# Adaptive layer norm block on one core: second half's means on 32-column tiles of TensorE, and the fifth product's operand prepared one step earlier

## The chip, the cores and the metric

The kernel is written in Bass and runs on one core of one Trainium2 chip. Everything is float32 in memory; the large products run in fp32r on pieces of the operands (high part and rest), the small ones in float32. The metric is the time of one execution on the device, in microseconds (us), the median of a few runs.

## The reference

```python
def reference(L0_attn_x, L0_ffn_W_gate, L0_ffn_W_up, L0_ffn_W_down, L0_c, L0_wmod):
    # x (2, 2048, 1024), W_gate and W_up (2752, 1024), W_down (1024, 2752), c (2, 1024), wmod (1024, 6144)
    x = L0_attn_x
    mod = (_silu(L0_c) @ L0_wmod).reshape(L0_c.shape[0], 6, 1, -1)
    sa, ca, ga, sb, cb, gb = (mod[:, 0], mod[:, 1], mod[:, 2], mod[:, 3], mod[:, 4], mod[:, 5])
    ga = (2 * (ga >= 0) - 1) * jnp.maximum(jnp.abs(ga), 0.25)
    gb = (2 * (gb >= 0) - 1) * jnp.maximum(jnp.abs(gb), 0.25)
    h = _layernorm(x, axis=-1) * (1 + ca) + sa
    x = x + ga * _L0_attn_ref(h)      # attention between the 2 batch rows, per channel, over the positions
    h = _layernorm(x, axis=-1) * (1 + cb) + sb
    x = x + gb * _L0_ffn_ref(h, L0_ffn_W_gate, L0_ffn_W_up, L0_ffn_W_down)   # silu(h Wg') * (h Wu'), then Wd'
    return x
```

The attention scores of a channel are sums over all 2048 positions, so the first layer norm has to be done for the whole of x before anything behind it can start.

## The kernel before

**Stages.** x lies with its features on the partitions and is cut into 8 chunks of 512 tokens (256 positions of both batch rows), 8 feature tiles of 128 each. Stage one normalises all chunks and gathers the sums for the attention; it takes four pairs of chunks in turns `t` = 0 and 1, each turn with pair `u` = 0 and 1 and chunk `h` = 0 and 1 of the pair. Stage two works out the attention's coefficients, applies them to the first two chunks, normalises again and makes the operands of the feed-forward part. Stage three, which is over nine tenths of the time, is the feed-forward part: products `P1` to `P7` of Strassen's scheme, each for two tiles of output features (`u` 0 and 1), three fp32r matmuls for each (high by high, high by rest, rest by high), then the down projection in the same manner. Every engine has its own program in written order; semaphores tie them together, so nothing is reordered.

**Stage one, turn t.** For a chunk, TensorE sums over the features by multiplying with ones, so that the mean stands on all 128 partitions (`means`, L1564: 8 float32 matmuls of 512 columns in turn 1). VectorE subtracts it (`centre`, L986, two instructions per chunk), ScalarE squares (`square`, L669), TensorE sums the squares on tiles of 32 columns, four quarters of the chunk side by side (`variances`, L1577), ScalarE takes the root (`root`, L677), VectorE the reciprocal (`invert`, L991), TensorE spreads it back over the partitions (`spread`, L1587, four matmuls with `rows_of`), VectorE multiplies (`normalise`, L1003) and takes the cross products (L1012), ScalarE the sums of squares of the result (`square_sums`, L686). VectorE's order in a turn is centre (0,0), (0,1), (1,0), invert (0,0), centre (1,1), invert (0,1), then the normalising of pair 0 and pair 1.

**Queues.** The sync engine (SP) issues the loads on queue q1: x, and the 24 parts of 1 MB of the modulation weights (`wmod`), which go through a ring of three buffers. Part w is loaded as soon as part w-3 has been multiplied (`parts`, L1535; `load_part`, L371). ScalarE issues the stores of the normalised chunks on its own queue q10 (`save_xhat`, L661), four halves of 2 MB in turn 0. Before it overwrites pair 1's buffer in turn 1, VectorE's centre (1,0) waits for the two stores of that pair (`xh_stored[1]`), and for all sums of squares of turn 0 (`sqsum_done`).

**The start of stage three.** The first pass takes the products in the order P1, P1, P2, P2, P5, P5, P6, P6, ... The operands of P1 and P2 are blocks of the normalised input (`raw_b11`, `raw_b21`), those of P5, P7, P6 and P4 sums of blocks. ScalarE makes the blocks of the second chunk (`modulate_f(1, k)`, L754, k 0 to 3 and then 4 to 7) and the high parts (`x_hi_first`, L794), VectorE the sums (L1220, L1224, L1231, L1234) and the rests (`x_lo_part`, L1193).

Of the kernel before, what the change touches and what calls it, by code (L numbers as in the profile page):

```python
# [20 lines left out]
F32 = mybir.dt.float32  # L21
# [4 lines left out]
P = 128  # L26
# [4 lines left out]
KD = D // P  # L31
KH = KD // 2
# [15 lines left out]
PRESUM = 4  # L48
NTB = T // P
# [81 lines left out]
def build(nc, x, xp, wgu, wgn, wdn, cT, eye, wmod, out):  # L131
# [3 lines left out]
    def sb(name, shape, dt, at):  # L135
        return nc.alloc_sbuf_tensor_at(name, [P] + shape, dt, offset=base + at)


    xbuf = [sb("xbuf0", [2, KD, NB, CC], F32, 32 * K), sb("xbuf1", [2, KD, NB, CC], F32, 64 * K)]
    dbuf = [sb("dbuf0", [2, KD, NB, CC], F32, 96 * K), sb("dbuf1", [2, KD, NB, CC], F32, 0)]  # L140
    rows_first = sb("rows_first", [2, BLOCK], F32, 140 * K)
    presum = sb("presum", [2, T], F32, 180 * K)
    presums = [presum, sb("presum1", [2, T], F32, 144 * K)]
# [120 lines left out]
    std_ready, inv_ready, rstd_ready = sem("std_ready"), sem("inv_ready"), sem("rstd_ready")  # L264
    xh_stored = [sem(f"xh_stored{u}") for u in range(2)]
    xhat_ready, sqsum_done, cross_done = sem("xhat_ready"), sem("sqsum_done"), sem("cross_done")
    wm_loaded = [sem(f"wm_loaded{r}") for r in range(WM_RING)]
    wm_last_loaded = sem("wm_last_loaded")
    silu_ready, mod_done = sem("silu_ready"), sem("mod_done")
# [47 lines left out]
    def tok(ap):  # L317

        return ap.rearrange("p k b c -> p k (b c)")
# [40 lines left out]
    with block as block:  # L360
# [281 lines left out]
        def _(act):  # L642
# [13 lines left out]
            for t in range(NPAIR // 2):  # L656
                def save_xhat(u, half):

                    act.wait_ge(xhat_ready, t * (4 * KD) + 2 * KD * u + KD * (half + 1))
                    first, ks = 4 * t + 2 * u + 2, slice(half * KD // 2, (half + 1) * KD // 2)  # L660
                    s.dma_start(xhat_dram[first:first + 2].rearrange("h p (k w) -> p h k w", k=KD)[:, :, ks],  # L661
                                tok2(dbuf[u][:, :, ks])).then_inc(xh_stored[u], 16)

                def square(u, h, js):
                    i = 2 * u + h
                    for j in js:
                        act.wait_ge(centred, t * 8 + (2 * i + j * 2 // NSQ + 1))
                        act.wait_ge(sq_used, t * (4 * NSQ) + (i * NSQ + j + 1))
                        s.activation(sq[:, j % 2], tok(dbuf[u][:, h])[:, j * SQ_PER:(j + 1) * SQ_PER, :], ACT.Square).then_inc(  # L669
                            sq_ready, 1)  # L670

                def root(u, h):
                    i = 2 * u + h
                    act.wait_ge(sq_used, t * (4 * NSQ) + (i * NSQ + NSQ + 2))
                    if t:
                        act.wait_ge(inv_ready, i + 1)
                    s.activation(std[:, u, h, :], ps_mean[u][h][:, 0:P], ACT.Sqrt, bias=eps_t, scale=1.0 / D).then_inc(std_ready, 1)  # L677

                def square_sums(u, ks):
                    for k in ks:  # L680
                        for b in range(NB):
                            n = 2 * u * KD + NB * k + b
                            act.wait_ge(xhat_ready, t * (4 * KD) + (n + 1))

                            act.wait_ge(sqsum_done, t * (4 * KD) + (4 * KD + n - 1))
                            s.activation(junk_a[:, b], dbuf[u][:, :, k, b, :], ACT.Square,  # L686
                                         accum_out=part[:, u, 2 + b, k:k + 1]).then_inc(sqsum_done, 1)

                for u, h in ((0, 0), (0, 1), (1, 0), (1, 1)):
                    square(u, h, range(NSQ // 2))  # L690
                    if (u, h) != (0, 0):
                        root(u if h else 0, 1 - h)
                    square(u, h, range(NSQ // 2, NSQ))
                root(1, 1)
                square_sums(0, range(KD // 2))
                save_xhat(0, 0)
                square_sums(0, range(KD // 2, KD))
                save_xhat(0, 1)
                if t:
                    copy_rows(0)  # L700
                square_sums(1, range(KD // 2))
                if t == 0:
                    save_xhat(1, 0)
                square_sums(1, range(KD // 2, KD - 2))
                if t:
                    copy_rows(1)
                square_sums(1, range(KD - 2, KD))
                if t == 0:
                    save_xhat(1, 1)
# [39 lines left out]
            def modulate_f(h, k):  # L749

                act.wait_ge(tf_ready, KD * h + k + 1)
                to = ((raw_b11, raw_b21), (x_raw["P6"], x_raw["P3"]))[h][k // KH]
                for n in range(NB):
                    ins = s.activation(to[:, k % KH, n * CC:(n + 1) * CC], xh_f[:, h, k, n, :], ACT.Identity,  # L754
                                       bias=mod[:, 3, n, k:k + 1], scale=cb1[:, n, k:k + 1])
                ins.then_inc(rawf_ready, 1)
# [26 lines left out]
            copy_rows(3)  # L783
            for m in range(4, EARLY):
                w_hi_cast(m)
            for k in range(KH, KD):
                modulate_f(1, k)

            def x_hi_first(name):

# [3 lines left out]
                s.copy(x_hi[name][:], x_raw[name][:]).then_inc(xhi_ready, 1)  # L794

            x_hi_first("P5")

            def silu_c11(g, u):

# [166 lines left out]
        def _(dve):  # L966
# [253 lines left out]
            v.tensor_tensor(x_raw["P5"][:], x_raw["P6"][:], raw_b11[:], ALU.subtract).then_inc(sumsf_ready, 1)  # L1220
            w_lo_part(3)
            w_lo_part(4)
            dve.wait_ge(rawf_ready, 2 * KD)
            v.tensor_tensor(x_raw["P7"][:], x_raw["P3"][:], x_raw["P6"][:], ALU.subtract).then_inc(sumsf_ready, 1)  # L1224
            x_lo_part(0, "P5")

            def x_first(i):

# [288 lines left out]
        def _(pe):  # L1517
# [36 lines left out]
            for t in range(NPAIR // 2):  # L1554
                def means(u, h):
                    i = 2 * u + h
                    pe.wait_ge(x_half, 16) if t == i == 0 else pe.wait_ge(x_loaded[u][h], t * 16 + 16)
                    if t and u == 0:
                        pe.wait_ge(std_ready, i + 1)
                    if t and u == 1:  # L1560
                        pe.wait_ge(xhat_ready, 2 * KD)
                    bank, ks = ps_mean_late[h] if t and u else ps_mean[u][h], range(KD) if t else range(PRESUM, KD) if i else range(KH)
                    for k in ks:
                        ins = mm(bank, ones[:], tok(xbuf[u][:, h])[:, k, :], start=k == ks[0], stop=t == 1 and k == KD - 1)  # L1564
                    if t == 0:
                        pe.wait_ge(presum_ready, i) if i else pe.wait_ge(half_ready, 2)
                        ins = mm(bank, ones[:], presums[u][:, h, :], start=False, stop=True)
                    ins.then_inc(mean_mm, 1)

                def variances(u, h):  # L1570
# [16 lines left out]
                        ins = mm(ps[:, RSTD_BANK[u] + h, b * P:(b + 1) * P], rows_of[:, b, :], inv[:, u, h, :], start=True, stop=True)  # L1587
                    ins.then_inc(rstd_ready, 1)

                means(0, 0)  # L1590
                means(0, 1)
                if t == 0:
                    means(1, 0)
                    variances(0, 0)
                    means(1, 1)
# [9 lines left out]
                    spread(1, 1)  # L1605
                    parts(0, range(2, 3))
                else:
                    means(1, 0)
                    means(1, 1)
                    parts(0, range(3, GROUP[0]))  # L1610
                    variances(0, 0)
                    variances(0, 1)
# [226 lines left out]
```

## Time and profile before

| | us |
|---|---|
| median of 3 runs | 2700.56 (2700.24 to 2702.29) |
| profiled execution | 2705.58 |
| its span | 2703.8 |
| TensorE busy in it | 2632.3 |
| VectorE busy | 1787.1 |
| ScalarE busy | 1303.8 |

The span runs from the first to the last instruction of the profiled execution, which took 1.78 us longer in all. Its own time is 5.02 us above the median of the unprofiled runs. TensorE is busy for 97% of the span. The exceptions lie in the first 215 us, stages one and two and the first products, where TensorE, VectorE, ScalarE and the transfers wait for each other.

### The profile page before, as it was taken

How to read it: one execution, taken by the hardware profiler on the slowest of the kernel's cores; microseconds unless marked ns; L12 is line 12 of the kernel's file. 1: busy time of each engine (PE TensorE's matmuls, PEld its weight loads, DVE VectorE, ACT ScalarE, POOL GpSimd, SP SyncE). 2: the span in 40 equal slices, each digit the busy share in tenths (PEclk: the TensorE clock that was granted, in tenths of full speed). 3: DMA queues.
4: the chain of work that ended last, by engine and by line, in shares of the span. 5: the costliest groups of instructions: out<-in, count | busy, mean ns of one | idle time of the engine just before them, and what ended most of it. 6: DMA issues, size and time to landing. Idle time of an engine off the chain costs nothing.

```text
span 2703.8 us, 34116 instructions
## 1 busy us (share of the span) xinstructions
PE 2632.3 (97%) x12264; PEld 2134.6 (79%) x12264; DVE 1787.1 (66%) x2505; ACT 1303.8 (48%) x2058; POOL 112.4 (4%) x176
## 2 busy tenths in 40 slices
PE   7779999999999999999999999999999999999999
PEld 3447888887888888888887888888888888888887
DVE  7898787758677757677757656667455555555544
ACT  5575555646555646456655333334333433343332
POOL 2000011010011010011000000000000000000000
PEclk9889999999999999999999999999999999999999
DMA  9764666567566557666559787778666667657655
GB/s 404 281 269 152 191 223 225 183 210 246 176 225 226 192 182 261 196 225 226 165 175 318 246 272 240 257 244 318 242 224 247 214 224 277 213 206 279 234 192 173
DMA packets 291432, 625.40 MB, mean 231 GB/s; under 512 B 22208, under 2 KB 91840, under 8 KB 285248
## 3 DMA queue, kind: packets, MB, share of 16 engines
q1 hardware_dynamic: 272544, 550.85, 59.4%
q0 software_dynamic: 17088, 59.78, 6.6%
q10 hardware_dynamic: 1632, 12.58, 1.1%
q8 instruction: 99, 1.62, 0.2%
q14 instruction: 69, 0.57, 0.1%
HBM read 437.79 MB, written 185.34 MB: 230 GB/s over the span
## 4 chain that ended last, share of the span: by engine, by line
PE 75%; DVE 1%; issue 0%; ACT 0%; DVEq 0%; ACTq 0%
PE ps L1711 15%; PE ps L1712 15%; PE ps L1713 15%; PE ps L1780 10%; PE ps L1781 10%; PE ps L1782 10%; DVE x_lo_P L1193 0%; DVE hl L1411 0%; DVE w_lo_P L1171 0%; PE ps L1722 0%; ACT w_hi L747 0%; PE ps L1721 0%; ACT x_hi_P L878 0%; DVE p L1360 0%; ACT w_hi L895 0%
## 5 line engine op out<-in xcount | busy, mean ns | idle before, releaser
L1711 PE MATMUL ps<-x_hi_P,w_hi 128*128 128x512 f32 x2416 | 943.9, 391 | 13.5 <-DVE x_lo_P L1193 5.4
L1712 PE MATMUL ps<-x_lo_P,w_hi 128*128 128x512 f32 x2416 | 942.5, 390 | 0.0
L1713 PE MATMUL ps<-x_hi_P,w_lo_P 128*128 128x512 f32 x2416 | 942.1, 390 | 0.0
L747 ACT CAST w_hi<-w_raw_P 128x512 fp32r<-128x512 f32 x604 | 374.4, 622 | 425.9 <-PE ps L1713 418.3
L1171 DVE TENSOR_TENSOR w_lo_P<-w_raw_P,w_hi 128x512 fp32r<-128x512 f32 x604 | 413.7, 686 | 206.3 <-PE ps L1713 183.7
L1711 PEld LDWEIGHTS ps<-x_hi_P,w_hi 128*128 128x128 f32 x2416 | 454.5, 188 | 112.2 <-issue 10.7
L1713 PEld LDWEIGHTS ps<-x_hi_P,w_lo_P 128*128 128x128 f32 x2416 | 454.7, 188 | 95.1
L1712 PEld LDWEIGHTS ps<-x_lo_P,w_hi 128*128 128x128 f32 x2416 | 454.9, 188 | 93.0
L1780 PE MATMUL ps<-hh,w_hi 128*128 128x512 f32 x1232 | 479.6, 389 | 0.5 <-DVE hb L1370 0.5
L1781 PE MATMUL ps<-hl,w_hi 128*128 128x512 f32 x1232 | 479.5, 389 | 0.0
L1782 PE MATMUL ps<-hh,w_lo 128*128 128x512 f32 x1232 | 479.5, 389 | 0.0
L1417 DVE TENSOR_TENSOR w_lo<-w_raw,w_hi 128x1408 fp32r<-128x1408 f32 x112 | 181.8, 1623 | 210.3 <-ACT w_hi L895 210.2
L895 ACT CAST w_hi<-w_raw 128x1408 fp32r<-128x1408 f32 x112 | 154.0, 1375 | 292.0 <-PE ps L1782 289.3
L1780 PEld LDWEIGHTS ps<-hh,w_hi 128*128 128x128 f32 x1232 | 231.3, 188 | 49.0 <-DVE hb L1370 0.9
L1782 PEld LDWEIGHTS ps<-hh,w_lo 128*128 128x128 f32 x1232 | 231.3, 188 | 48.0
L1781 PEld LDWEIGHTS ps<-hl,w_hi 128*128 128x128 f32 x1232 | 231.3, 188 | 47.8
L1411 DVE TENSOR_TENSOR hl<-hl_raw,hh 128x1536 fp32r<-128x1536 f32 x112 | 179.0, 1619 | 5.1 <-ACT hh L888 5.0
L888 ACT CAST hh<-hl_raw 128x1536 fp32r<-128x1536 f32 x112 | 150.7, 1370 | 6.4 <-DMA hl_raw<-h_dram 6.4
L1363 DVE TENSOR_TENSOR ww<-ps,ww 128x512 f32<-128x512 f32 x84 | 58.0, 690 | 98.6 <-ACT ww L830 97.0
L830 ACT COPY ww<-ps 128x512 f32<-128x512 f32 x84 | 49.1, 585 | 98.4 <-PE ps L1713 93.9
L824 ACT COPY vv<-ps 128x512 f32<-128x512 f32 x84 | 49.1, 584 | 97.2 <-PE ps L1713 97.1
L1366 DVE TENSOR_TENSOR vv<-ps,vv 128x512 f32<-128x512 f32 x84 | 57.9, 689 | 54.7 <-PE ps L1713 54.0
(188 smaller groups left out, 1966.6 us busy)
## 6 DMA issues: line engine op xcount, KB each, us to landing
w_raw_P<-wgu SPq DMA_DIRECT2D x294, 256.0 KB, 3.0
w_raw_P<-wsum_dram SPq DMA_DIRECT2D x252, 256.0 KB, 3.7
hl_raw<-h_dram SPq DMA_DIRECT2D x84, 768.0 KB, 7.6
w_raw<-wds_dram SPq DMA_DIRECT2D x64, 704.0 KB, 4.6
h_dram<-hb SPq DMA_DIRECT2D x33, 1280.0 KB, 5.6
w_raw<-wdn SPq DMA_DIRECT2D x48, 704.0 KB, 5.3
wsum_dram<-w_raw_P SPq DMA_DIRECT2D x84, 256.0 KB, 3.1
x_raw_P<-xr_dram SPq DMA_DIRECT2D x21, 1024.0 KB, 12.0
```

Source lines behind the costliest of these rows:

```text
L747: s.copy(w_hi[m % HI_RING][:], w_raw[(name, u)][:]).then_inc(whi_ready, 1)
L888: s.copy(hh[stage % 2][:, j0:j1, :], hl_raw[stage % 2][:, j0:j1, :]).then_inc(hh_ready, 1)
L895: s.copy(w2_hi[b % 4][:], w2_raw[b % 4][:]).then_inc(w2hi_ready, 1)
L1171: v.tensor_tensor(w_lo[(name, u)][:], w_raw[(name, u)][:], w_hi[m % HI_RING][:].bitcast(F32), ALU.subtract).then_inc(w_ready, 1)
L1411: v.tensor_tensor(hl[stage % 2][:, j0:j1, :], hl_raw[stage % 2][:, j0:j1, :], hh[stage % 2][:, j0:j1, :].bitcast(F32), ALU.subtract).then_ ...
L1417: v.tensor_tensor(w2_lo[b % 4][:], w2_raw[b % 4][:], w2_hi[b % 4][:].bitcast(F32), ALU.subtract).then_inc(w2_ready, 1)
L1711: mm(to, hi[:, w], xh, start=fresh and k == 0, stop=False, skip_group_check=not fresh)
L1712: mm(to, hi[:, w], xl, start=False, stop=False, skip_group_check=not fresh)
L1713: ins = mm(to, lo[:, w], xh, start=False, stop=k == KH - 1, skip_group_check=not fresh)
L1780: mm(bank, hi[:, w], hh[stage % 2][:, j, :], start=fresh and j == 0, stop=False, skip_group_check=not fresh)
L1781: mm(bank, hi[:, w], hl[stage % 2][:, j, :], start=False, stop=False, skip_group_check=not fresh)
L1782: ins = mm(bank, lo[:, w], hh[stage % 2][:, j, :], start=False, stop=j == NPT - 1, skip_group_check=not fresh)
```

## The change

Two things change. In turn 1 the means are summed by quarters: four matmuls of 128 columns for each feature tile, on tiles of 32 columns of the array, as the variances are. The result is one row in each quarter of a bank, which ScalarE copies to `mean_q`, and four matmuls with `rows_of` spread it over the partitions of the bank that VectorE reads. At the start of stage three, ScalarE casts the operand of P5 ahead of the second half of `modulate_f(1, k)`, and VectorE takes its rest ahead of the sum for P7.

```diff
@@ ScalarE, turn 0 of stage one
                 square_sums(1, range(KD // 2))
                 if t == 0:
                     save_xhat(1, 0)
+                    for u in range(2):
+                        for h in range(2):
+                            act.wait_ge(quarters_made, 2 * u + h + 1)
+                            s.copy(mean_q[:, u, h, :], (ps_mean_late[h] if u else ps_mean[u][h])[:, 0:P]).then_inc(quarters_copied, 1)
                 square_sums(1, range(KD // 2, KD - 2))
@@ ScalarE, start of stage three
-            for k in range(KH, KD):
-                modulate_f(1, k)
...
             x_hi_first("P5")
+            for k in range(KH, KD):
+                modulate_f(1, k)
@@ VectorE, start of stage three
             w_lo_part(3)
             w_lo_part(4)
+            x_lo_part(0, "P5")
             dve.wait_ge(rawf_ready, 2 * KD)
             v.tensor_tensor(x_raw["P7"][:], x_raw["P3"][:], x_raw["P6"][:], ALU.subtract).then_inc(sumsf_ready, 1)
-            x_lo_part(0, "P5")
@@ TensorE, stage one (the old means(u, h) stays for turn 0 alone)
+                def quarter_means(u, h):
+                    i = 2 * u + h
+                    bank = ps_mean_late[h] if u else ps_mean[u][h]
+                    pe.wait_ge(x_loaded[u][h], 32)
+                    pe.wait_ge(xhat_ready, 2 * KD) if u else pe.wait_ge(std_ready, i + 1)
+                    for k in range(KD):
+                        for b in range(NTB):
+                            ins = mm(bank[b * QP:(b + 1) * QP, 0:P], ones[:, 0:QP], tok(xbuf[u][:, h])[:, k, b * P:(b + 1) * P],
+                                     start=k == 0, stop=k == KD - 1)
+                    ins.then_inc(quarters_made, 1)
+
+                def spread_means(u, h):
+                    pe.wait_ge(quarters_copied, 2 * u + h + 1)
+                    bank = ps_mean_late[h] if u else ps_mean[u][h]
+                    for b in range(NTB):
+                        ins = mm(bank[:, b * P:(b + 1) * P], rows_of[:, b, :], mean_q[:, u, h, :], start=True, stop=True)
                     ins.then_inc(mean_mm, 1)
...
-                means(0, 0)
-                means(0, 1)
                 if t == 0:
+                    means(0, 0)
+                    means(0, 1)
...
                 else:
-                    means(1, 0)
-                    means(1, 1)
+                    for u, h in ((0, 0), (0, 1), (1, 0), (1, 1)):
+                        quarter_means(u, h)
+                    for u, h in ((0, 0), (0, 1), (1, 0), (1, 1)):
+                        spread_means(u, h)
                     parts(0, range(3, GROUP[0]))
                     variances(0, 0)
```

The order of TensorE's instructions where turn 1 begins, before (`wm` are the ring's buffers, `xbuf_49` and `xbuf_50` the two pairs; the last of each row is the shape of one and how many stand in a row):

```order
L1535 MATMUL ps<-wm_58,silu_pad 32x256 x8
L1564 MATMUL ps<-xbuf_49,ones 128x512 x16
L1564 MATMUL ps<-xbuf_50,ones 128x512 x16
L1535 MATMUL ps<-wm_56,silu_pad 32x256 x8
L1535 MATMUL ps<-wm_57,silu_pad 32x256 x8
L1535 MATMUL ps<-wm_58,silu_pad 32x256 x8
L1577 MATMUL ps<-sq,ones 32x128 x64
```

And the same place after the change:

```order
L1541 MATMUL ps<-wm_59,silu_pad 32x256 x8
L1577 MATMUL ps<-xbuf_49,ones 32x128 x64
L1577 MATMUL ps<-xbuf_50,ones 32x128 x64
L1585 MATMUL ps<-mean_q,rows_of 128x128 x16
L1541 MATMUL ps<-wm_57,silu_pad 32x256 x8
L1541 MATMUL ps<-wm_58,silu_pad 32x256 x8
L1541 MATMUL ps<-wm_59,silu_pad 32x256 x8
L1595 MATMUL ps<-sq,ones 32x128 x64
```

The 32 matmuls over all columns became 128 on tiles and 16 that spread; the three parts of the modulation and the variances still follow in that order.

ScalarE's order around its stores of turn 0, after the change:

```order
L688 ACTIVATE junk_a,part<-dbuf_52 128x512 x8
L663 DMA xhat_dram<-dbuf_52 128x2x2048
L709 COPY mean_q<-ps 128x128 x4
L688 ACTIVATE junk_a,part<-dbuf_52 128x512 x8
L663 DMA xhat_dram<-dbuf_52 128x2x2048
```

The four copies stand between the third store and the second half of pair 1's sums of squares, ahead of the fourth store; before there was nothing between.

VectorE's order at the start of stage three, before (L1220 is the sum for P5, L1224 the one for P7, L1193 the rest of P5's and, further down, of P6's operand):

```order
L1220 TENSOR_TENSOR x_raw_P_100<-x_raw_P_101,raw_b_94 128x2048
L1171 TENSOR_TENSOR w_lo_P_1_140<-w_raw_P_1_126,w_hi_148 128x512
L1171 TENSOR_TENSOR w_lo_P_0_133<-w_raw_P_0_119,w_hi_149 128x512
L1224 TENSOR_TENSOR x_raw_P_102<-x_raw_P_98,x_raw_P_101 128x2048
L1193 TENSOR_TENSOR x_lo_P_107<-x_raw_P_100,x_hi_P_114 128x2048
L1360 TENSOR_TENSOR p_0_150<-ps,p_0_150 128x512
L1171 TENSOR_TENSOR w_lo_P_1_134<-w_raw_P_1_120,w_hi_145 128x512
L1231 TENSOR_TENSOR x_raw_P_101<-x_raw_P_102,raw_b_94 128x2048
```

And after:

```order
L1226 TENSOR_TENSOR x_raw_P_101<-x_raw_P_102,raw_b_95 128x2048
L1177 TENSOR_TENSOR w_lo_P_1_141<-w_raw_P_1_127,w_hi_149 128x512
L1177 TENSOR_TENSOR w_lo_P_0_134<-w_raw_P_0_120,w_hi_150 128x512
L1199 TENSOR_TENSOR x_lo_P_108<-x_raw_P_101,x_hi_P_115 128x2048
L1231 TENSOR_TENSOR x_raw_P_103<-x_raw_P_99,x_raw_P_102 128x2048
L1366 TENSOR_TENSOR p_0_151<-ps,p_0_151 128x512
L1177 TENSOR_TENSOR w_lo_P_1_135<-w_raw_P_1_121,w_hi_146 128x512
L1237 TENSOR_TENSOR x_raw_P_102<-x_raw_P_103,raw_b_95 128x2048
```

The rest of P5's operand and the sum for P7 changed places; all behind them stands as before.

## Rows read from the trace of the kernel before

**Rows 1.** The page's head: span of the profiled execution.

```profile
span 2703.8 us, 34116 instructions
```

**Rows 2.** Timeline, TensorE: start, duration (us), line, shapes, records, [idle before <- releaser].

```profile
42.37 1.05 PE L1535 MATMUL ps<-wm,silu_pad 128*32 128x256 f32 x16
43.23 1.21 PE L1577 MATMUL ps<-sq,ones 128*32 128x128 f32 x32
...
46.61 1.16 PE L1587 MATMUL ps<-inv,rows_of 128*128 128x128 f32 x8
...
55.20 27.73 PE L1564 MATMUL ps<-xbuf,ones 128*128 128x512 f32 x64
82.86 2.80 PE L1535 MATMUL ps<-wm,silu_pad 128*32 128x256 f32 x48
...
96.65 2.05 PE L1587 MATMUL ps<-inv,rows_of 128*128 128x128 f32 x8 [2.60 <-issue]
```

**Rows 3.** Timeline, VectorE, 70 to 99 us.

```profile
70.23 8.88 DVE L986 SCALAR_TENSOR_TENSOR dbuf<-ps,xbuf 128x2048 f32<-128x2048 f32 x4
79.61 4.49 DVE L986 SCALAR_TENSOR_TENSOR dbuf<-ps,xbuf 128x2048 f32<-128x2048 f32 x2 [0.49 <-DMA xhat_dram<-dbuf]
90.40 0.95 DVE L991 RECIPROCAL inv<-std 128x128 f32<-128x128 f32 x1 [6.30 <-ACT std L677]
...
98.81 0.69 DVE L1003 SCALAR_TENSOR_TENSOR dbuf<-ps,dbuf 128x512 f32<-128x512 f32 x1 [2.16 <-PE ps L1587]
```

**Rows 4.** Timeline, ScalarE, 46 to 70 us (ACTq: an issued transfer).

```profile
46.75 0.37 ACT L677 ACTIVATE std<-ps,eps_pair 128x128 f32<-128x128 f32 x1 [0.76 <-PE ps L1577]
...
61.81 0.61 ACT L686 ACTIVATE junk_a<-dbuf 128x512 f32<-128x512 f32 x1
...
63.01 0.63 ACT L686 ACTIVATE junk_a<-dbuf 128x512 f32<-128x512 f32 x1 [0.50 <-DVE dbuf L1003]
...
69.14 0.37 ACTq L661 DMA_DIRECT2D xhat_dram<-dbuf  x1
```

**Rows 5.** Timeline, SP's queue, 55 to 56 us: the load of part 5.

```profile
55.33 0.33 SPq L371 DMA_DIRECT2D wm<-wmod  x1
```

**Rows 6.** DMA queues, 58 to 59 us: packets, MB, share of 16 engines.

```profile
q1 hardware_dynamic: 10, 0.07, 15.6%
```

**Rows 7.** DMA queues, 59 to 60 us.

```profile
q1 hardware_dynamic: 28, 0.22, 52.2%
q10 hardware_dynamic: 23, 0.19, 44.4%
```

**Rows 8.** DMA queues, 72 to 80 us: all that moved.

```profile
q10 hardware_dynamic: 313, 2.32, 68.6%
```

**Rows 9.** DMA queues, 68.2 to 80 us: all that moved.

```profile
q10 hardware_dynamic: 517, 3.94, 79.0%
```

**Rows 10.** Timeline, ScalarE, 197 to 203 us.

```profile
197.13 4.05 ACT L754 ACTIVATE x_raw_P<-dbuf,mod,cb 128x256 f32<-128x256 f32 x8
201.09 1.89 ACT L794 CAST x_hi_P<-x_raw_P 128x2048 fp32r<-128x2048 f32 x1
```

**Rows 11.** Timeline, VectorE, 195 to 213 us.

```profile
195.43 2.29 DVE L1220 TENSOR_TENSOR x_raw_P<-x_raw_P,raw_b 128x2048 f32<-128x2048 f32 x1
...
201.21 2.29 DVE L1224 TENSOR_TENSOR x_raw_P<-x_raw_P,x_raw_P 128x2048 f32<-128x2048 f32 x1 [2.29 <-ACT x_raw_P L754]
203.42 2.28 DVE L1193 TENSOR_TENSOR x_lo_P<-x_raw_P,x_hi_P 128x2048 fp32r<-128x2048 f32 x1
...
212.54 2.29 DVE L1193 TENSOR_TENSOR x_lo_P<-x_raw_P,x_hi_P 128x2048 fp32r<-128x2048 f32 x1
```

**Rows 12.** Timeline, TensorE: the first matmul of P5 and of P6.

```profile
205.85 0.77 PE L1711 MATMUL ps<-x_hi_P,w_hi 128*128 128x512 f32 x1 [3.34 <-DVE x_lo_P L1193]
...
214.98 0.47 PE L1711 MATMUL ps<-x_hi_P,w_hi 128*128 128x512 f32 x1 [2.02 <-DVE x_lo_P L1193]
```

**Rows 13.** Windows: stretch, length, busy time by engine, granted clock (PEclk), DMA.

```profile
216.00:219.00 3.00, 3.00 (x9) 2.32 (x8) 3.00 (x3) 0.77 (x1) 0.00 (x0) 0.50 0.00 0
```

More of the change, by code:

```diff
@@ L140, in build @@
     dbuf = [sb("dbuf0", [2, KD, NB, CC], F32, 96 * K), sb("dbuf1", [2, KD, NB, CC], F32, 0)]
+    mean_q = sb("mean_q", [2, 2, P], F32, 136 * K)
     rows_first = sb("rows_first", [2, BLOCK], F32, 140 * K)
@@ L266, in build @@
     xhat_ready, sqsum_done, cross_done = sem("xhat_ready"), sem("sqsum_done"), sem("cross_done")
+    quarters_made, quarters_copied = sem("quarters_made"), sem("quarters_copied")
     wm_loaded = [sem(f"wm_loaded{r}") for r in range(WM_RING)]
@@ L1556, in means @@
                     i = 2 * u + h
[L1557 to L1562, printed above, removed]
-                    for k in ks:
[L1564 to L1567, printed above, removed]
+                    pe.wait_ge(x_loaded[u][h], 16) if i else pe.wait_ge(x_half, 16)
+                    bank, ks = ps_mean[u][h], range(PRESUM, KD) if i else range(KH)
+                    for k in ks:
+                        mm(bank, ones[:], tok(xbuf[u][:, h])[:, k, :], start=k == ks[0], stop=False)
+                    pe.wait_ge(presum_ready, i) if i else pe.wait_ge(half_ready, 2)
+                    mm(bank, ones[:], presums[u][:, h, :], start=False, stop=True).then_inc(mean_mm, 1)
+                def quarter_means(u, h):
[13 more added lines that the diff above has]
+                        ins = mm(bank[:, b * P:(b + 1) * P], rows_of[:, b, :], mean_q[:, u, h, :], start=True, stop=True)
                     ins.then_inc(mean_mm, 1)
```

## The prediction

> **What bounds the kernel now.** I first read the page. TensorE is busy for nearly the whole span of 2703.8 us [rows 1], with the products above all. Nothing in the change touches a product's matmuls, so it can win or lose only where TensorE is not the bound: before about 215 us. There I read the timelines of the engines side by side, asking at each idle stretch what ended it. A microsecond saved there that reaches the first products is a microsecond of the whole, since all behind them follows at TensorE's own pace.
>
> In turn 1 of stage one TensorE sums the means without a pause from 55.20 for 27.73 us, then does three modulation parts, 2.80 us, and only then the variances [rows 2]. VectorE has meanwhile subtracted the means of three chunks: (0,0) and (0,1) from 70.23, 8.88 us, and (1,0) from 79.61, 4.49 us. Then it stands for 6.30 us until the first root arrives at 90.40 [rows 3]. The root waited for ScalarE's squares, these for the variances, and these for TensorE, which still had the means of pair 1 and the parts ahead of them. From 90.40 on everything in stages one and two hangs on this reciprocal: it, centre (1,1), the second reciprocal, the spread, and the normalising at 98.81 [rows 3]. So 6.30 us is what faster means can bring here at most. The 20 us by which the sums get shorter are not the measure.
>
> Directly ahead of it is a smaller wait: centre (1,0) could not start before 79.61, and waited 0.49 us for the store of the normalised pair 1 [rows 3]. Today that wait costs nothing, for the engine stands 6.30 us afterwards. It is the wait that comes next.
>
> **The means on tiles.** A modulation part is 8 matmuls of 256 columns on 32-column tiles; two neighbours start 0.86 us apart (42.37 to 43.23) [rows 2]. A chunk's quarters are 32 matmuls of 128 columns on such tiles, twice the columns: 1.72 us, against 27.73/4 = 6.93. All four take 6.9 us, 55.20 to 62.1. The Trainium skill, in "TensorE: Matmul & The Clock Gate", section "Why this matters for your kernels", gives 3.07 times for four tiles of 32 rows and 2.38 times for three of 32 columns, less than the four times that the row shows here. An estimate by its 3.07 is 2.26 us per chunk, 64.2 instead of 62.1, and that would move the loads below by about 2 us to later, and so make the gain 1 us larger.
>
> The copies: ScalarE has issued sum 8 of pair 1 at 61.81 and is free at about 62.5 [rows 4]. Four copies of 128 by 128 out of a bank, each like the root of the same shape, 0.37 us [rows 4], take until 64.0, and none waits. The next sum of squares begins 1.0 us late (64.0 for 63.01), but VectorE feeds these sums more slowly than ScalarE does them, 0.50 us of waiting for each feature tile [rows 4]. Two tiles later the delay is gone, ahead of the fourth store at 69.14 [rows 4]. Cost nothing; without that cover it is 1.5 us. Behind the copies on ScalarE stand only those sums, the store and the squares, and the squares wait for VectorE's centring anyway.
>
> The spreads: four times 1.16 us [rows 2], the first at 62.9 once the first copy is made, the last done at 67.5. VectorE wants the first mean at 70.23 [rows 3]: hidden, by 6 us for the first one. Of the 16 added matmuls nothing is on the path.
>
> Now the parts follow at 67.5 instead of 82.86, and the variances at about 70.3, then at VectorE's pace. The first root is ready before centre (1,0) ends, so the 6.30 us wait is gone whole. VectorE goes from 79.61 straight on, and its reciprocal would be at 84.1.
>
> **What the earlier parts trigger.** Each finished part frees a buffer of the ring, and SP issues the next load. The first part of the three ends at 67.5 + 2.80/3 = 68.4, so parts 6, 7 and 8, 3.15 MB, are asked for from 68.4 on, not from 84. At that time queue q10 still has the stores of pair 1 to move: 3.94 MB after 68.2, 2.32 MB after 72 [rows 8, 9]. Before, the loads came when the stores had long landed. How do the two queues share? Part 5 was issued at 55.33 [rows 5] into a running store. At 58 to 59 q1 moved 0.07 MB [rows 6], at 59 to 60 0.22 MB beside q10's 0.19 [rows 7]: a start 3.7 us after the issue, and then halves. So q1 takes half from 72.1 on, when 2.32 MB of the stores are left. The engines move about 0.41 MB per us (rows 7 together). 2.32 MB alone take 5.6 us, at half the rate 11.2. The stores land 5.6 us later, centre (1,0) starts at 85.2 and not at 79.61, and the wait of 0.49 becomes one of 6.1. The reciprocal comes at 89.7. Gain: 90.40 - 89.7 = **0.7 us** of the 6.30. Behind centre (1,0) on VectorE stand both reciprocals and centre (1,1), and the spread, TensorE and ScalarE wait for them; this is why the whole delay counts.
>
> Bounds: no delay of the stores, 6.3 us gained; all three loads ahead of the rest of the stores, 3.15/0.41 = 7.7 us of delay, 1.4 us lost. I take equal halves, since rows 7 show just this pair of queues in just this state.
>
> The Trainium skill, "DMA: Bandwidth & Descriptors", section "Queues, rings and completion order", says that each engine goes in turn between the queues that have work, a packet at a time. By that rule the stores get no precedence for being earlier, and it speaks against this change as rows 7 do; the sum would be the same.
>
> **The fifth product's operand.** P5 waited 3.34 us for its rest and started at 205.85; P6 waited 2.02 and started at 214.98 [rows 12]. Now ScalarE casts P5's high part once VectorE's sum is there, 195.43 + 2.29 = 197.7, until 199.6, and modulates the second half from 199.6 to 203.6, 2.4 us later than before (197.13 to 201.2) [rows 10, 11]. VectorE takes P5's rest from 199.7 to 201.9, so P5 follows the turn ahead of it at 202.5: its 3.34 us are gone. But the sum for P7 needs the second half of the modulation: 203.65 for 201.21. P5's rest, 2.2 us on VectorE, no longer stands behind it [rows 11], so what follows, up to P6's rest at 212.54, comes 2.44 - 2.2 = 0.25 us later. P6 starts at 215.2. All that P5 wins TensorE spends waiting for P6, about 5.3 us, part of it ahead of P5's second tile, whose weights are split in the same VectorE queue. Cost: **0.25 us**, between 0 and 0.6 (0.6 is ScalarE's own delay by the wait for the sum, 197.7 for 197.1).
>
> TensorE's clock: after the wait ahead of P6 it ran at 0.50 at 216 to 219 [rows 13], that is 1.2 GHz, and so did the spread after the 2.60 us idle, 2.05 us for 1.16 [rows 2]. Longer idle ahead of both places now can make such a stretch begin earlier; the most that it can cost at P6 is another stretch like that, 3 us at half speed, 1.5 us; the least nothing, since the stretch is there already. I take 0.2, near the low end.
>
> **Sum.** The profiled execution: 2705.58 - 0.7 + 0.25 + 0.2 = 2705.3. It lies 5.02 us above the median of the unprofiled runs, and a difference made at the start carries over: 2700.56 - 0.25 = **2700.3 us**. A measurement of this kernel can tell 0.2% from no change, 5.4 us: below 2695.2 or above 2706.0.
>
> **Rivals.**
> *The stores are not held up* (the loads start after 77, or q10 keeps its rate). Then 6.3 us are gained and 0.45 lost: 2694.7. For it: at 58 to 59 q1 got 0.07 MB only, with its load already issued [rows 6]. Against it: rows 7, one microsecond later. Any half-way case lies between; each microsecond that the loads start later gives one back. Chance 0.17.
> *The loads overtake the stores.* Place: centre (1,0). They land 7.7 us later, the reciprocal is at 91.8, 1.4 us later than now, and with the 0.45 the time is 2702.4. It decides from a start of centre (1,0) at 85.5 on, which is only 0.3 us behind my forecast. For it: 3.94 MB are on the way when the loads are issued [rows 9]; against it, halves in rows 7. With the whole extra stretch at 1.2 GHz it is 2703.7. Chance 0.12.
> *P5's gain is kept* (P6's operand is not the next bound): 3.3 us more, 2697.0. Against it: VectorE goes without a gap from the sum at 201.21 to the rest of P6 at 212.54 [rows 11]. Chance 0.03.
> *The tiles do not overlap, or the means run at 1.2 GHz.* Not overlapping, the fourth quarter is ready at 82.8, ScalarE holds back half its sums and the fourth store till then, and centre (1,0) comes some 15 us late, some 10 us lost: 2710. Against it: the variances and parts on such tiles [rows 2]. At 1.2 GHz the quarters end at 69.0; that costs ScalarE 5 us but also starts the loads later, and ends within 3 us of no change. Chance 0.04 for both.
> My forecast, a late store that eats most of the gain, has 0.64.
>
> **Range and chances.** The cases within 2 us of no change and the overtaking one lie from 2698.5 to 2703.8; the rival at 2694.7 has 0.17, and I reach nearly to it: 2695.0 to 2703.8. Of its 0.17 about 0.11 is below 2695.2, with 0.03 for what I don't see: faster 0.14. Slower by over 0.2% needs the tiles to fail or something that I don't see: 0.05. Within: 0.81.
>
> **What the profile of after would show.** The quarters done at about 62, copies on ScalarE at 62.5 to 64, parts at 67.5; the loads of parts 6 to 8 issued at 68 to 71, both queues at half from 72 on; centre (1,0) waiting some 6 us for the store, and no wait ahead of the first reciprocal, at 89 to 90; P5 with no wait, P6 with about 5 us. It is wrong if centre (1,0) starts near 80, if the copies hold the fourth store, or if P6 starts earlier, counted from P1's first matmul, than now.

## The result, and the profile after

| | before | after |
|---|---|---|
| median of 20 runs each (us) | 2702.15 (2699.12 to 2703.96) | 2705.66 (2702.56 to 2708.81) |
| ratio to before | | 1.0015, 95% interval 1.0009 to 1.0021 |
| profiled execution | 2705.58 | 2703.47 |
| its span | 2703.8 | 2701.7 |

The changed kernel is slower by 3.5 us by the medians, 0.15% by the ratio (which is worked out from all the runs and is not the quotient of the medians): inside the 0.2% that the chances call "same", but 5.4 us above the predicted 2700.3 and above the end of the range, 2703.8. The two profiled executions say the opposite, 2.1 us faster. The one of before was slower than each of the 20 runs of before, the one of after is 2.2 us under its own median. This disagreement is the way into the mistake, as the experiments show.

TensorE's timeline in the profile of after, the new means and what follows them (columns as in [rows 2]; all lines have moved, by 20 here):

```profile
55.02 7.39 PE L1577 MATMUL ps<-xbuf,ones 128*32 128x128 f32 x224
63.78 1.08 PE L1577 MATMUL ps<-xbuf,ones 128*32 128x128 f32 x32 [1.37 <-issue]
64.79 3.84 PE L1585 MATMUL ps<-mean_q,rows_of 128*128 128x128 f32 x32
68.56 2.80 PE L1541 MATMUL ps<-wm,silu_pad 128*32 128x256 f32 x48
```

The tiles do overlap: the sums that took 27.73 us [rows 2] end at 64.9 instead of 82.9. 62.1 was predicted, from a pace of 1.72 us per chunk. The pace was right: in the profile of e11 below, at 2.4 GHz (granted clock 1.00 from 54 to 58 us), the first three and a half chunks take 6.30 us. Two things came on top in after. TensorE began the sums at 1.2 GHz (granted clock 0.59 from 54 to 58 us, 1.00 after that), and it paused for 1.37 us within the fourth chunk. The profile names no wait for the pause. It is there in all eight profiles with the new means, 1.37 to 1.90 us long, and in after one packet of instructions was moved just ahead of it (queue, kind: packets, MB, share, 61.5 to 62 us):

```profile
q8 instruction: 1, 0.02, 11.6%
```

Whether TensorE was waiting for these instructions was not tested. The parts begin at 68.56 (predicted 67.5), and the next loads leave at once. SP's queue, and then the DMA queues from 74 to 76 us (packets, MB, share of 16 engines):

```profile
69.69 2.40 SPq L373 DMA_DIRECT2D wm<-wmod  x3
```

```profile
q1 hardware_dynamic: 56, 0.46, 54.1%
q10 hardware_dynamic: 53, 0.40, 47.4%
```

Before, q10 had these microseconds for itself [rows 8]. The Trainium skill, "DMA: Bandwidth & Descriptors", section "Queues, rings and completion order", lets each engine go in turn between the queues that have work; the trace agrees, with 0.46 MB beside 0.40. VectorE's timeline, which answers to [rows 3]:

```profile
70.01 8.88 DVE L992 SCALAR_TENSOR_TENSOR dbuf<-ps,xbuf 128x2048 f32<-128x2048 f32 x4
84.69 4.49 DVE L992 SCALAR_TENSOR_TENSOR dbuf<-ps,xbuf 128x2048 f32<-128x2048 f32 x2 [5.80 <-DMA xhat_dram<-dbuf]
89.09 0.94 DVE L997 RECIPROCAL inv<-std 128x128 f32<-128x128 f32 x1
...
97.48 0.69 DVE L1009 SCALAR_TENSOR_TENSOR dbuf<-ps,dbuf 128x512 f32<-128x512 f32 x1 [2.16 <-PE ps L1605]
...
106.10 0.95 DVE L997 RECIPROCAL inv<-std 128x128 f32<-128x128 f32 x1 [3.64 <-ACT std L679]
```

The 6.30 us ahead of the reciprocal are gone, and 5.80 us of waiting for the store of pair 1 stand ahead of centre (1,0). The reciprocal comes at 89.09 for 90.40, 1.3 us earlier. At 106.10 nothing of it is left (105.76 before): the third reciprocal waits 3.64 us for its root.

The last of ScalarE's copies (answering to [rows 4]) waited 2.16 us for the chunk with the pause, but the fourth store left at 69.02, for 69.14:

```profile
62.20 0.58 ACT L709 COPY mean_q<-ps 128x128 f32<-128x128 f32 x3
64.93 0.27 ACT L709 COPY mean_q<-ps 128x128 f32<-128x128 f32 x1 [2.16 <-PE ps L1577]
...
69.02 0.37 ACTq L663 DMA_DIRECT2D xhat_dram<-dbuf  x1
```

TensorE at P1, at P5, at P5's second tile and at P6 (answering to [rows 12]):

```profile
186.09 0.47 PE L1731 MATMUL ps<-x_hi_P,w_hi 128*128 128x512 f32 x1 [1.83 <-DVE x_lo_P L1194]
...
201.35 0.47 PE L1731 MATMUL ps<-x_hi_P,w_hi 128*128 128x512 f32 x1
...
206.41 0.50 PE L1731 MATMUL ps<-x_hi_P,w_hi 128*128 128x512 f32 x1 [2.06 <-DVE w_lo_P L1177]
...
214.43 0.77 PE L1731 MATMUL ps<-x_hi_P,w_hi 128*128 128x512 f32 x1 [3.42 <-DVE x_lo_P L1199]
215.00 0.63 PE L1732 MATMUL ps<-x_lo_P,w_hi 128*128 128x512 f32 x1
```

P5 no longer waits. P6 starts 28.34 us after P1, against 28.11 in the profile of before (214.98 [rows 12] less 186.87, where P1's first matmul stood): 0.23 us later, and 0.25 was predicted. So this pair of profiles bears out nearly every step, and the runs still say 3.5 us slower.

### The profile page after: what moved, and what is told of

It reads as the page before. It is cut to its first block and busy times, and to the rows that moved or that the text cites. A ratio compares the mean times of both kernels' runs of the same rounds, so it can differ in the third digit from the quotient of the medians.

```text
span 2701.7 us, 34568 instructions
## 1 busy us (share of the span) xinstructions
PE 2617.3 (97%) x12488; PEld 2134.9 (79%) x12488; DVE 1786.5 (66%) x2505; ACT 1304.0 (48%) x2062; POOL 112.4 (4%) x176
```

## The experiments

Each kernel was timed beside the kernel before on the same chip, and profiled once. The ratio is to before; the medians of before were 2701.28 us beside e1 to e4, 2701.86 beside e5 to e8 and 2701.28 beside e9 to e11.

| | what it is | median | ratio, 95% | P1 at | P5 | P6 | P6, tile 2 | profiled |
|---|---|---|---|---|---|---|---|---|
| before | | | | 186.87 | 18.98 | 28.11 | 32.53 | 2705.58 |
| e4 | before again | 2700.67 | 0.9997 (0.9988 to 1.0006) | 187.42 | 17.39 | 26.52 | 29.32 | 2701.74 |
| after | | 2705.66 | 1.0015 (1.0009 to 1.0021) | 186.09 | 15.26 | 28.34 | 32.69 | 2703.47 |
| e1 | means alone | 2702.94 | 1.0009 (1.0000 to 1.0017) | 187.32 | 17.35 | 26.48 | 29.29 | 2702.32 |
| e11 | means alone, again | 2702.51 | 1.0005 (0.9996 to 1.0014) | 188.80 | 18.95 | 28.09 | 30.89 | 2705.81 |
| e2 | P5's edit alone | 2705.49 | 1.0014 (1.0005 to 1.0023) | 186.52 | 15.27 | 28.35 | 33.32 | 2706.76 |
| e3 | means, parts late | 2696.42 | 0.9983 (0.9974 to 0.9991) | 180.46 | 18.96 | 28.09 | 30.91 | 2696.72 |
| e9 | means, loads held | 2697.41 | 0.9986 (0.9977 to 0.9994) | 181.17 | 18.98 | 28.11 | 30.92 | 2697.58 |
| e5 | cast of P5 in between | 2702.79 | 1.0001 (0.9992 to 1.0009) | 186.43 | 15.27 | 26.60 | 31.01 | 2701.88 |
| e6 | e2, gaps filled | 2704.18 | 1.0005 (0.9996 to 1.0014) | 186.56 | 15.27 | 28.35 | 31.19 | 2703.39 |
| e7 | after, parts late | 2699.40 | 0.9988 (0.9979 to 0.9996) | 180.67 | 15.27 | 28.34 | 32.69 | 2699.40 |
| e8 | after, both mends | 2697.82 | 0.9985 (0.9976 to 0.9994) | 179.41 | 16.60 | 27.94 | 32.26 | 2697.68 |
| e10 | e3, gaps filled | 2696.87 | 0.9983 (0.9974 to 0.9992) | 181.41 | 17.37 | 26.50 | 30.91 | 2698.46 |

"P1 at" is the start of P1's first matmul in TensorE's timeline; the next three columns are the starts of P5, P6 and P6's second tile counted from it. All times are in us. From P6's second tile to the end the profiled executions take 2484.4 to 2486.9 us more: 2485.6 on average in the six with the old order of P5 and no filling, 2485.9 in after, e2 and e7. So the edits show ahead of that tile, and behind it lies a spread of 2.5 us that no edit explains. Of the 2.1 us by which the profile of after is the faster one, 1.5 lie there.

**e1 and e2: each half alone.** e1 is the changed kernel with P5's edit undone; e2 is the kernel before with that edit alone, and the old means:

```diff
@@ ScalarE (e2; e1 has the old order here)
-            for k in range(KH, KD):
-                modulate_f(1, k)
...
             x_hi_first("P5")
+            for k in range(KH, KD):
+                modulate_f(1, k)
@@ VectorE
+            x_lo_part(0, "P5")
             dve.wait_ge(rawf_ready, 2 * KD)
             v.tensor_tensor(x_raw["P7"][:], x_raw["P3"][:], x_raw["P6"][:], ALU.subtract).then_inc(sumsf_ready, 1)
-            x_lo_part(0, "P5")
```

> Only the tiled means, the P5 operand left as before. Theory A (the P5 edit costs: longer idle of TensorE ahead of P6 brings more 1.2 GHz stretches on average than the one profile showed): about 1 us below the kernel before. Theory B (the means cost: TensorE idle and at 1.2 GHz for much of 80 to 100 us, or a store that lands later than in the profile): 3 us above it. In the profile both expect centre (1,0) to wait about 5.8 us for the store and P5 to wait about 3.3 us as before.

> Only the P5 operand moved, the means as before. Theory A: 3 to 4 us above the kernel before, with P6 some 28.3 us after P1's first matmul and idle of 5 us in two waits ahead of it, and products at 1.2 GHz for longer. Theory B: 0.2 to 0.5 us above, within what can be told from no change.

e1 is 1.7 us slower by the medians, with an interval that touches 1, between what the two theories gave it; e2 is 4.2 us slower, clearly, as theory A has it. The halves sum to 5.9 for the 3.5 of the whole change, which their intervals (0 to 4.6 us and 1.4 to 6.2 us) allow. The edit priced at 0.25 us carries most of the loss. In e1, VectorE's wait for the store and SP's loads:

```profile
85.71 4.49 DVE L992 SCALAR_TENSOR_TENSOR dbuf<-ps,xbuf 128x2048 f32<-128x2048 f32 x2 [6.67 <-DMA xhat_dram<-dbuf]
90.12 0.94 DVE L997 RECIPROCAL inv<-std 128x128 f32<-128x128 f32 x1
```

```profile
68.63 2.05 SPq L373 DMA_DIRECT2D wm<-wmod  x3
```

In e2, ScalarE's timeline where the cast now stands, and TensorE's where P6 begins:

```profile
194.64 0.62 ACT L747 CAST w_hi<-w_raw_P 128x512 fp32r<-128x512 f32 x1
197.40 1.92 ACT L792 CAST x_hi_P<-x_raw_P 128x2048 fp32r<-128x2048 f32 x1 [2.14 <-DVE x_raw_P L1220]
199.21 4.06 ACT L754 ACTIVATE x_raw_P<-dbuf,mod,cb 128x256 f32<-128x256 f32 x8
```

```profile
214.87 0.76 PE L1711 MATMUL ps<-x_hi_P,w_hi 128*128 128x512 f32 x1 [4.96 <-DVE x_lo_P L1193]
215.43 0.63 PE L1712 MATMUL ps<-x_lo_P,w_hi 128*128 128x512 f32 x1
```

ScalarE is free at 195.26 and stands 2.14 us for the sum of P5, with the modulation behind it. The prediction had it free at 197.13, when the sum was nearly there.

**e4: the kernel before, again.** Unchanged, for a second profile of it.

> The kernel before, unchanged, for a second profile: the ratio is 1 within 0.1%. The distance from P1's first matmul to the end of P6's and the time at 1.2 GHz ahead of 230 us show how far they differ from one execution to the next; theory A expects P1 to end of P6 to vary by under 1 us here.

The same place on ScalarE, first in the profile of before, then in e4:

```profile
196.12 0.59 ACT L654 COPY presum<-ps 128x512 f32<-128x512 f32 x1 [1.56 <-PE ps L1535]
196.60 0.62 ACT L747 CAST w_hi<-w_raw_P 128x512 fp32r<-128x512 f32 x1
```

```profile
195.09 0.57 ACT L654 COPY presum<-ps 128x512 f32<-128x512 f32 x1
195.55 0.62 ACT L747 CAST w_hi<-w_raw_P 128x512 fp32r<-128x512 f32 x1
196.07 4.06 ACT L754 ACTIVATE x_raw_P<-dbuf,mod,cb 128x256 f32<-128x256 f32 x8
```

In the first, ScalarE waited 1.56 us for TensorE's modulation parts behind P1. They came late because P1 had run in part at half speed. TensorE's timeline of before, and its window from 188.4 to 191.6 us (columns as in [rows 13]):

```profile
188.09 0.41 PE L1713 MATMUL ps<-x_hi_P,w_lo_P 128*128 128x512 f32 x1
188.72 0.63 PE L1712 MATMUL ps<-x_lo_P,w_hi 128*128 128x512 f32 x1
...
194.12 1.93 PE L1535 MATMUL ps<-wm_late,silu_pad 128*32 128x256 f32 x32
```

```profile
188.40:191.60 3.20, 3.20 (x9) 2.52 (x8) 3.20 (x7) 3.20 (x6) 0.00 (x0) 0.50 0.03 13
```

And the parts in e4, where all of P1's matmuls are short:

```profile
193.05 1.93 PE L1535 MATMUL ps<-wm_late,silu_pad 128*32 128x256 f32 x32
```

A matmul of P1 takes 0.39 at 2.4 GHz and 0.63 at 1.2 GHz. The parts start 7.25 us after P1 in before and 5.63 us in e4. In e4 ScalarE has no wait, and P6 starts 26.52 us after P1 for 28.11. Theory A had expected the stretch from P1 to the end of P6 to vary by under 1 us; up to P6's second tile it varies by 3.2. Its timeline at P6, to be set against e2's:

```profile
213.94 0.47 PE L1711 MATMUL ps<-x_hi_P,w_hi 128*128 128x512 f32 x1 [1.80 <-DVE x_lo_P L1193]
214.25 0.39 PE L1712 MATMUL ps<-x_lo_P,w_hi 128*128 128x512 f32 x1
```

**e5: the wait taken out of P5's edit.** Before, with VectorE's edit, and ScalarE's cast placed behind the sixth feature tile instead of ahead of the fifth:

```diff
+            for k in range(KH, KD - 2):
+                modulate_f(1, k)
             x_hi_first("P5")
+            for k in range(KD - 2, KD):
+                modulate_f(1, k)
```

> On the kernel before: VectorE as with the P5 operand moved, but ScalarE casts P5 between feature tiles 5 and 6 of the second modulation half and not ahead of tile 4. Theory A1 (ScalarE standing 2.1 us for the sum of P5 is what makes P6's operand late): no wait there, P6 starts 26.1 to 26.5 us after P1's first matmul instead of 28.35, and the time is within 1 us of the kernel before, maybe 0.5 below. Theory A2 (any cast ahead of the end of the modulation costs its full 1.8 us): P6 at 28 us or later and the time 2 to 4 us above.

ScalarE's cast and TensorE's P6 in e5:

```profile
197.31 1.92 ACT L792 CAST x_hi_P<-x_raw_P 128x2048 fp32r<-128x2048 f32 x1
```

```profile
213.03 0.62 PE L1713 MATMUL ps<-x_hi_P,w_hi 128*128 128x512 f32 x1 [5.01 <-DVE x_lo_P L1195]
```

The cast runs at the same time as in e2, but with two feature tiles of modulation done in what was the wait. P6 is back at 26.60 (26.1 to 26.5 expected), P5 keeps its early start, and the time is within 1 us of before, although P6's first tile still takes 4.41 us (31.01 less 26.60). The win of P5 buys nothing, as predicted: TensorE spends it waiting 5.01 us for P6's operand.

**e6: the clock's part.** e2, with useless matmuls in the idle time: 8 ahead of P5's second tile and 20 ahead of P6 (the counts in `FILL`), into a bank that is free then.

```diff
+                if g == 0 and (name, u) in FILL:
+                    for _ in range(FILL[(name, u)]):
+                        mm(ps[:, 6, :], ones_r[:], x_hi["P1"][:, 0, :], start=True, stop=True)
                 product(m)
```

> The P5 operand moved as in the change, the means as before, and TensorE does matmuls without use into a free bank while it waits (8 ahead of P5's second tile, 20 ahead of P6). If of the 4 us some 2 are products at 1.2 GHz after the two waits: no stretch at 1.2 GHz at P6, P6's first tile takes 2.8 us and not 4.3 to 5.0, and the time is 1.5 to 2.5 us below that of the P5 operand moved alone. If the loss is all in the late operand: the same time as there.

TensorE's timeline in e6:

```profile
209.78 4.69 PE L1745 MATMUL ps<-x_hi_P,ones_r 128*128 128x512 f32 x20
214.91 0.47 PE L1712 MATMUL ps<-x_hi_P,w_hi 128*128 128x512 f32 x1 [0.43 <-DVE x_lo_P L1194]
215.21 0.39 PE L1713 MATMUL ps<-x_lo_P,w_hi 128*128 128x512 f32 x1
```

P6 starts as late as in e2, but its first tile takes 2.84 us (31.19 less 28.35) for 4.97. The time falls by 1.9 us (2.3 above before, for e2's 4.2). The intervals of e2 and e6 overlap, so the runs alone don't prove it; the timelines show where 2.1 us come from.

**e3 and e9: the late store.** e3 is e1 with the three parts behind the variances of pair 0, so that the next loads leave late. e9 keeps the parts early and holds only the load of part 6 until pair 1 is stored:

```diff
@@ e3, TensorE
-                    parts(0, range(3, GROUP[0]))
                     variances(0, 0)
                     variances(0, 1)
+                    parts(0, range(3, GROUP[0]))
@@ e9, SP's load_part
+                if w == GROUP[0]:
+                    sp.wait_ge(xh_stored[1], 32)
```

> Only the tiled means, and in turn 1 the three modulation parts 3 to 5 moved behind variances (0,1), so that the loads of parts 6 to 8 are issued at about 82 us, when the stores have landed. If the loads hold the store up (shown by the wait of 5.8 us): centre (1,0) starts near 79.5 again, the first reciprocal at 84 to 85, and the time is 4 to 6 us below that of the tiled means alone. If the store is late for another reason: the wait of 5 to 6 us stays and the time is that of the tiled means alone.

> The tiled means alone, the parts at their early place, but SP holds the load of part 6 until both stores of pair 1 have landed. If it is the loads in the transfer queues that hold the stores up, and not the early parts on TensorE: centre (1,0) starts near 79.3, the first reciprocal near 83.6, and the time is that of the tiled means with late parts, 6 us below the tiled means alone. If the early parts or variances on TensorE matter by themselves: the wait of 6 us stays.

VectorE in e3, then VectorE and SP's queue in e9:

```profile
79.14 4.49 DVE L992 SCALAR_TENSOR_TENSOR dbuf<-ps,xbuf 128x2048 f32<-128x2048 f32 x2 [0.19 <-DMA xhat_dram<-dbuf]
83.54 0.94 DVE L997 RECIPROCAL inv<-std 128x128 f32<-128x128 f32 x1
```

```profile
79.59 4.49 DVE L994 SCALAR_TENSOR_TENSOR dbuf<-ps,xbuf 128x2048 f32<-128x2048 f32 x2 [0.63 <-DMA xhat_dram<-dbuf]
84.00 0.94 DVE L999 RECIPROCAL inv<-std 128x128 f32<-128x128 f32 x1
```

```profile
79.55 1.28 SPq L375 DMA_DIRECT2D wm<-wmod  x3
```

They bring the reciprocal 6.9 and 6.4 us forward (90.40 before), and start P1 6.4 and 5.7 us earlier than before's profile. In e9 the parts run at 67.64, near e1's 67.50, and only the loads are late: it is their traffic that holds the store, and not TensorE's order. The time falls by 4.9 and 3.9 us, and lies 6.5 and 5.5 us under e1's, where 4 to 6 and 6 were expected.

**e7 and e8: the whole change with mends.** e7 is after with e3's order of the parts; e8 has e5's placement of the cast as well.

> The whole change with the three modulation parts behind variances (0,1). If the two halves of the change add up: 4 us above the tiled means with late parts, so 1 us below the kernel before, 5 to 6 us below the change as made.

> The whole change with both mends: parts behind variances (0,1), and P5's cast between tiles 5 and 6 of the modulation. Theory A1: as fast as the tiled means with late parts or 0.5 us faster, 5 us below the kernel before. Theory A2: 2 to 4 us slower than that.

e7 is 2.5 us faster than before (1 was expected), where e3 without P5's edit is 4.9 faster. With the cast in between it is 4.0 faster (5 expected). By the medians the edit costs 2.4 us here too, but the intervals of e7, e8 and e3 overlap.

**e10: e3 with 9 matmuls to fill ahead of P5 and 7 ahead of P6.**

> The tiled means with late parts, P5's operand as in the kernel before, and matmuls without use into a free bank ahead of P5 (9) and P6 (7), to keep TensorE at 2.4 GHz through both waits. If the stretch at 1.2 GHz inside P5 lies under the cover of P6's operand, and only one inside P6 costs: 0 to 1 us below the same kernel without them, since P6's first tile ran at 2.4 GHz there in the one profile. The fastest kernel here either way.

It is as fast as e3, to 0.5 us, where up to 1 us faster was expected. P5 runs at 2.4 GHz, but P6's first tile takes 4.41 us (30.91 less 26.50), with 8 of its 12 matmuls at 0.59 to 0.63, for 2.82 in e3. It waits 1.86 us behind the 7 matmuls; P6 of e3, whose P1 and P5 ran slower, waits 0.61. TensorE in e10:

```profile
207.91 0.47 PE L1732 MATMUL ps<-x_hi_P,w_hi 128*128 128x512 f32 x1 [1.86 <-DVE x_lo_P L1200]
```

**e11: e1 again**, for a second profile of the means.

> The tiled means alone a second time, since the first left open whether they cost 0 or 4 us. If the late store eats the gain and nothing else happens: within 1 us of the kernel before. If the means cost something of their own: 2 us or more above it again.

VectorE's timeline and SP's queue in e11:

```profile
86.80 4.49 DVE L992 SCALAR_TENSOR_TENSOR dbuf<-ps,xbuf 128x2048 f32<-128x2048 f32 x2 [7.83 <-DMA xhat_dram<-dbuf]
91.20 0.94 DVE L997 RECIPROCAL inv<-std 128x128 f32<-128x128 f32 x1
```

```profile
67.47 2.12 SPq L373 DMA_DIRECT2D wm<-wmod  x3
```

Three profiles of the same means differ in when the loads leave, and the store follows: loads at 69.69, 68.63 and 67.47, centre (1,0) at 84.69, 85.71 and 86.80. Over these three, each microsecond that the loads are earlier makes the store 0.95 us later. The time, 1.2 us above before, again lies between the two cases of the expectation.

## Why the prediction was wrong

**The means: mechanism right, size about 2 us too favourable.** That the store takes the place of the wait, that the loads of parts 6 to 8 cause it, and that some 6.3 us are there to be won, is shown by e3 and e9. The forecast was 0.7 us of gain. The loads left at other times than the predicted 68.4, and the prediction moves centre (1,0) by as much the other way: 83.9, 85.0 and 86.1 for after, e1 and e11. It started at 84.69, 85.71 and 86.80, 0.7 to 0.8 us later. So the delay of the store was sized that much too short. At the first reciprocal the three have 89.09, 90.12 and 91.20, mean 90.1, and gain 0.2 us against the mean of 90.3 in the five profiles with the old means (before, e2, e4, e5, e6).

At P1 nothing is left: 186.09, 187.32 and 188.80, mean 187.4, against 186.4 to 187.4, mean 186.8, in the five. From the first reciprocal to P1 the three take 97.0, 97.2 and 97.6 us, the five 96.2 to 96.9 (e3 and e9, with the loads late, 96.9 and 97.2). The prediction carried a gain at the reciprocal to P1 whole; some 0.8 us more were lost on the way, and the cause of that stays open. TensorE is at half speed for much of the time in which it has little to do (the windows from 82 to 100 us, columns as in [rows 13], first after, then before):

```profile
82.00:100.00 18.00, 7.36 (x60) 5.26 (x64) 13.16 (x16) 2.46 (x4) 0.00 (x0) 0.57 0.17 71
```

```profile
82.00:100.00 18.00, 12.83 (x215) 8.23 (x217) 9.54 (x9) 8.19 (x10) 0.00 (x0) 0.91 0.47 177
```

But that is not enough for an explanation. After gives back its 1.3 us by the third reciprocal, 17.0 us behind the first, with the modulation parts and the sums of squares ahead of it in part at half speed; e4, with the old means, takes 16.9 us for the same, and e1 and e11, with granted clocks of 0.59 and 0.65 in this window, take 15.8 and 15.6, near before's 15.4.

The runs say 1.2 to 1.7 us slower, with intervals that touch no change. "The loads overtake the stores" decided from a start of 85.5 on: e1 and e11 are beyond it, after is not. Forecast and rival were one mechanism with two issue times, and 0.12 was too little for that rival.

**The copies and spreads: right.** They cost nothing that shows, even with a copy 2.16 us late: the fourth store left on time, and VectorE took the first mean at 70.01 without a wait.

**The fifth product's operand: this step failed.** "Cost: 0.25 us, between 0 and 0.6", and 0.2 for the clock. The order of events was right, as was "all that P5 wins TensorE spends waiting for P6". The cost was worked out from ScalarE's start at 197.13 [rows 10]. That start was already 1.56 us late in this one execution, because P1 had fallen to 1.2 GHz. This delay covered the wait that the cast adds. When P1 keeps its clock, ScalarE is free some 2 us before the sum, the cast makes it stand (2.14 us in e2), and P6 starts 28.35 us after P1 for 26.52: 1.83 us, not 0.25. All four profiles with the cast at this place (after, e2, e6, e7) have P1 at 2.4 GHz and P6 at 28.34 or 28.35. None shows the edit behind a slow P1, for which the prediction's sum would give 28.36.

The clock's term failed for the same reason. Behind the longer idle P6's first tile takes 4.97 us in e2 (granted clock 0.50 from 215.4 to 219.2 us) and 4.35 in after and e7, against 2.80 to 2.82 in five of the six profiles with the old order and 4.42 in the one that I read. I took 0.2 "since the stretch is there already"; it was there in that profile alone.

The size that one profile could not give: P6's second tile begins, after P1, at 32.53, 29.32, 29.29, 30.89, 30.91 and 30.92 in the six profiles with the old order (before, e4, e1, e11, e3, e9), mean 30.6, and at 32.69, 33.32 and 32.69 with the edit (after, e2, e7), mean 32.9. That is 2.3 us: 0.8 from P6's later start (28.3 against a mean of 27.6) and 1.5 from its first tile (4.6 against 3.1). The profile of before is the latest of its six; from it the same difference is 0.4. The three with the edit all happen to have P1 at 2.4 GHz; against e4 and e1, the two old ones that have it too, the difference is 3.6. The runs give 3.8 us for e2 (1.4 to 6.2), and 2.4 between e7 and e3. In e5, with the wait taken out, P6 starts 1.75 us earlier than in e2 and the time is 0.9 us above before for 4.2. The timelines thus show the wait as the cause of P6's late start; by the runs alone the intervals of e2 and e5 still touch.

**The sum.** The difference was forecast as -0.25 us and is +3.5. P5's two terms were 1.9 to 3.4 us short (2.3 to 3.8 for 0.45) and the means' 1.9 to 2.4, together enough for the 3.75 between, and not told apart more finely than that. The other 1.6 us of the distance to 2700.3 are the base: the median of before is 2702.15 in 20 runs, 2700.56 in the first three. "A difference made at the start carries over" is borne out, within the spread of 2.5 us named above. But the 5.02 us between the profile and the median, which I only subtracted, were a warning that this execution was unlike the others in some stretch. It was in the very one that I read: its P6's second tile comes 2.7 us later than in e4.

**Open.** What costs 0.8 us between the first reciprocal and P1 with the new means, and what makes the profiled executions differ by up to 2.5 us behind P6's second tile. Of the 3.8 us between those of before and e4, 2.7 are there by that tile (186.87 + 32.53 = 219.40 for 187.42 + 29.32 = 216.74) and 1.2 arise behind it. The runs' 3.8 us for e2 can't be divided more finely than this allows.

**The best version** is e3, the new means with the parts behind the variances and P5's operand as before: 2696.42 us, 0.9983 (0.9974 to 0.9991), 4.9 us faster than before. e8, e9 and e10 are not to be told from it, and e7's interval overlaps its.

## What to carry to other kernels

When one engine gets faster, list the transfers that its progress releases, and look for a store on another queue that something waits for at that time; here moving three parts of 0.9 us each back turned 1.2 to 1.7 us lost into 4.9 won. A step put ahead of others on an in-order engine costs the time from when the engine is free to when the step's input is there, so read "free" from more than one execution: here a clock that fell by chance in one profile hid a wait that the edit brings in others. If the profiled execution stands clear of the median, take a second profile of the same kernel before costing an edit of a microsecond.

## What the runs showed of the hardware that was not expected

Four chunks' sums on 32-column tiles, 128 matmuls in place of 32, took 7.39 + 1.08 us of busy time in after for 27.73, over three times faster, though part of it ran at 1.2 GHz. At 2.4 GHz throughout, in e11, it was 6.30 + 1.08 us.

The same kernel falls to 1.2 GHz at different places in different executions. P1 did so in four of the six profiles with the old order of P5, and each time P6 began 1.6 us later, though P2 began only 0.4 us later. P1 ended 1.6 us later (its last matmul starts 6.94 us after its first in before, 5.32 in e4), which made the parts behind it late, and through ScalarE and VectorE the operand of P6.

In after the granted clock was 0.57 from 82 to 100 us, where TensorE had little to do, and the first spread there, behind 7.24 us of idle, took 2.05 us; before, with work up to its start, it took 1.16 (92.89 to 94.05). A stage that got shorter left TensorE idle, and what came next ran at half speed. That this costs time in the end is not shown: e1 and e11 reach the third reciprocal within 0.4 us of before's distance.
